# A graph transformer layer: when the edge histogram is built beside the keys and values, and when the last weight split and the attention row loads are issued

## The chip, the cores and the metric

The kernel runs on one core of a Trainium2 chip. The metric is the device time of the whole program in microseconds. The core has TensorE (PE, matrix products), VectorE (DVE), ScalarE (ACT), GpSimd (POOL) and the DMA queues, of which SyncE (SP) issues most. The engines run their own instruction lists in order and meet only at semaphores.

## The reference, cut to what matters

The layer takes 1250 nodes of 768 features and 41250 directed edges (self loops included). In outline:

```python
xn = layernorm(x)
# graph branch: two attention layers over the edges, src -> dst
h  = (layernorm(xn, g, b) @ W1).reshape(n, 4, 192)
e  = leaky_relu(s_src[src] + s_dst[dst], 0.2)
alpha = exp(e - segment_max(e)) / segment_sum(...)
out1 = segment_sum(alpha * h[src], dst) ; out2 = same with W2
gnn  = concat(x, out2) @ Wu + bu
# linear attention branch
q, k = elu(xn @ Wq + bq) + 1, elu(xn @ Wk + bk) + 1 ;  v = xn @ Wv + bv
kv = sum_n k v ; mix = (q kv / (q sum k)) @ Wo + bo
x = x + gnn + mix
x = x + mixture_of_experts(layernorm(x))      # top 2 of 8
```

## The kernel before, in words

All rows of x are cut into NT = 10 tiles of 128 rows, and features into KC = 6 blocks of 128. Large products are done in three half-precision passes: each operand is split into a high and a low part, so `product` (line 1931) issues 18 matmuls for one half of a tile. The high part of a weight is made by ScalarE (`high`, line 971), the low part by VectorE (`stage_low`, line 1330), each in CUTS = 3 pieces.

The edges are turned into a dense 1280x1280 table of counts, `CT`, by a histogram. The edges come in NU = 81 units of 512. For each unit VectorE writes four pairs of one-hot matrices (lines 1394 and 1395), TensorE multiplies them (four matmuls, line 2032) and VectorE adds the result of 240 columns to a window of `CT` (`edges_add`, line 1387). VectorE's order is fixed: after the one-hots of unit u it adds unit u-2, and it waits there for TensorE. The ring of one-hots has OB = 4 places. On TensorE unit u waits for the one-hots of u and for the add of u-2, since two PSUM banks (4 and 5) are used in turn.

The units are laid between the steps of two stages by `spread(step)`:

- **The key and value stage** has KV_STEPS = 36 steps. In round t (0 to 9) TensorE does two half products of values of tile t, two half products of keys of tile t+2, each followed by one step of units, and then 12 small matmuls that add k times v (line 2043). FIRST names the first step that takes units, KVU how many of the 81 are done in this stage. VectorE does in the same rounds the units, `key_biased` (line 1344, out of the banks of the keys), `key_features` (lines 1349, 1350), the low parts of expert weights (`conv_low`, line 1335) and from round 4 on a low part of the folded weight `MG` (line 1425). Tile 1 of the keys sits in banks 4 and 5 until `key_biased(1)` has read it.
- **The G stage** has 20 half products, each with one step of the units that are left.

Then come six products by Wo (line 2100), and the query stage: for each j of 6, TensorE does a half product of queries (18 matmuls, 512 columns), small denominator products of the block before (`den`, line 2113, which wait for `QT` of that block) and turns a piece of the edge mask (line 2159). ScalarE makes exp and relu of the queries and a high part of an expert weight, VectorE makes `QT` (line 1511), the low part of the expert weight (line 1335) and, in blocks 0, 1 and 2, one piece each of the low part of Wu (line 1330). From block 4 on VectorE also takes row maxima (`maxima1`, line 1492), and the first of them waits for four broadcast loads of the attention rows from `as_d` (line 716). SP issues those loads after it has served the expert pieces of block 2 and a store of the mask. After the last block TensorE does the graph half products, the first of which stands before `den(5)`.

The order of the work is written out by hand. No planner is in it.

Of the kernel before, what the change touches and what calls it, by code (L numbers as in the profile page):

```python
# [23 lines left out]
def gps_layer(nc, x, src, dst, norm_g, norm_b, W1, a_src1, a_dst1, b1, W2, a_src2, a_dst2, b2, Wu, bu,  # L24
# [27 lines left out]
    with ctx:  # L52
# [371 lines left out]
        s_k_biased = sem("k_biased")  # L424
# [86 lines left out]
        s_y_ready = sem("y_ready")  # L511

        KV_STEPS = 4 * NT - 4
        KVU = 54
        assert KVU <= NU
        xs_in = (s_x0_in, s_x1_in, s_x2_in, s_x3_in, s_x4_in, s_x5_in)
        convs_in = (s_ring0_in, s_ring1_in, s_ring2_in, s_ring3_in)
# [14 lines left out]
        CONST = 10  # L532
        CUTS = 3
        BLANK = 3600
        FIRST = 2
        AHEAD = 4
        FIRST_AT = {0: (4,), 1: (5, 6), 2: (7, 8), 3: (9, 10), 4: (11,)}
        KEY_AT = {4: (0, 0), 5: (0, 1), 6: (1, 0), 7: (1, 1)}
# [41 lines left out]
        def _(sp):  # L580
# [126 lines left out]
            for n, (c0, w) in enumerate(CH):  # L707
                for j in range(KC):
                    i = n * KC + j
                    convs(conv_of_j[i])  # L710
                    mask_stores(HALF_J.get(i, ()))
                    if i == CUTS - 1:
                        sp.wait_ge(s_cols_out, 16)
                        sp.wait_ge(s_stage_low, 4 * CUTS)
                        for h in range(H1):
                            sp.dma_start(arow1[h], as_d[h * NP:(h + 1) * NP].partition_broadcast(P)).then_inc(s_arow_in, 16)
                if n == len(CH) - 1:
                    sp.wait_ge(s_cols_ready, 2)
                    sp.dma_start(rr_d.rearrange("(r p) -> r p", p=P), rowst[0:2 * H1 * NT, :]).then_inc(s_cols_out, 16)
                    sp.wait_ge(s_max_done, H1 * NT)  # L720
                    sp.dma_start(WUB[0:KS], Wu[D:D + CW, :].rearrange("(k p) n -> p k n", p=KS)).then_inc(s_w2_in, 16)
                    sp.wait_ge(s_small_in, 96)
                    sp.dma_start(WUB[KS:KS + 1, 0, :], bias_d.rearrange("(a n) -> a n", a=1)).then_inc(s_w2_in, 16)
                    for b in (2, 3):
                        sp.wait_ge(convs_out[b], CONVS[b])
                    sp.dma_start(reg(O_G, 2 * GW), g_d[:, 0:2 * GW]).then_inc(s_gbuf0, 16)
                    sp.wait_ge(s_cols_out, 32)
                    rr_load(0)
                t0 = c0 // P
                for t in range(t0, (c0 + w) // P):  # L730
                    convs(conv_of_t[t])
                    if t == t0:
                        if t:
                            xa_load(t + 1)
                        continue
                    if t == t0 + 1:
                        xa_store(t0)
                    mask_stores(HALF_T.get(t, ()))
                    if t < NT - 1:
                        xa_load(t + 1)  # L740
                    else:
                        sp.wait_ge(s_zq_ready, NJ)
                        rr_load(1)
                        for b in range(2):
                            sp.wait_ge(masks_out[b], 16 * ((NT + 1 - b) // 2))
                        sp.wait_ge(xa_out[0], XAS)
                        sp.dma_start(reg(O_G + 2 * GW, 3 * GW), g_d[:, 2 * GW:5 * GW]).then_inc(s_gbuf1, 16)
                    xa_store(t)
# [476 lines left out]
        def _(dve):  # L1225
# [65 lines left out]
            with dve.If(some > 0):  # L1291

                with dve.Fori(0, NWIN) as w:
# [17 lines left out]
                    with dve.Fori(0, NU) as u:  # L1311
                        dve.wait_ge(s_left_step, w * LW + LW)
                        for j in range(EJ):
                            V.tensor_scalar(ohleft[:, j, :], iota[:, 0:P], kc[:, 1, j, bass.ds(u, 1)], None, ALU.is_equal)
                            i = V.tensor_scalar(ohk[:, 0, j, :], iota[:, 0:NT * W], kc[:, 0, j, bass.ds(u, 1)], None, ALU.is_equal)
# [189 lines left out]
            for n, (c0, w) in enumerate(CH):  # L1505
                for j in range(KC):
                    i = n * KC + j
                    dve.wait_ge(s_q_act, i + 1)
                    if c0:
                        dve.wait_ge(s_acc_psum, c0 // P)  # L1510
                    V.scalar_tensor_tensor(QT[:, j, 0:w], EQ[:, i % 3, 0:w], 1.0, RQ[:, i % 2, 0:w],
                                           ALU.min, ALU.add).then_inc(s_q_ready, 1)
                    for c in conv_of_j[i]:
                        conv_low(c)
                    if i < CUTS:
                        stage_low(3, i)
                    if i in IND_J:
                        edge_or_not(IND_J[i])
                    if j < KC - 1:
                        maxima1(MAX_J.get(i, ()))  # L1520
                    if i == NJ - KC + 1:
                        columns1()

                t0 = c0 // P
                dve.wait_ge(s_den_psum, 2 * n + 1)
                nt = w // P
                heads = recip[:, 0:nt, :]
                link(V.reciprocal(heads, ps[2][:, 0:nt * 2 * KC].rearrange("p (t h) -> p t h", t=nt)))
                for r in range(3):
                    part = rcols[:, 0:nt, 2 * KC * r:2 * KC * (r + 1)]  # L1530
                    k = V.tensor_copy(part, heads)
                    if r < 2:
                        link(k)
                        link(V.tensor_tensor(heads, heads, part, ALU.subtract))
                k.then_inc(s_den_ready, 1)
                for c in conv_of_t[t0]:
                    conv_low(c)
                late_maxima = MAX_J.get(n * KC + KC - 1, ())
                maxima1(late_maxima[0:1])
                dve.wait_ge(s_den_psum, 2 * n + 2)  # L1540
                V.tensor_copy(rparts[:, 0:w], ps[2].bitcast(BF16)[:, 2 * P:2 * P + w]).then_inc(s_den_ready, 1)
                maxima1(late_maxima[1:])

                def zq_low(i):
                    dve.wait_ge(s_zqh_ready, i + 1)
                    V.tensor_tensor(ZQ[:, i % KC, 1, 0:w], EQ[:, i % 3, 0:w], ZQ[:, i % KC, 0, 0:w], ALU.subtract).then_inc(s_zq_ready, 1)

                for j in range(KC):
                    i = n * KC + j
                    dve.wait_ge(s_bc_psum, i + 1)  # L1550
                    if j == 0:
                        dve.wait_ge(s_q_ready, (n + 1) * KC)
                    elif j >= 3:
                        dve.wait_ge(s_zq_ready, i - 2)
                    V.tensor_tensor(EQ[:, i % 3, 0:w], QT[:, j, 0:w], ps[i % 2][:, 0:w], ALU.mult).then_inc(s_z_ready, 1)
                    if j:
                        zq_low(i - 1)
                zq_low(n * KC + KC - 1)

                def acc_out(t):  # L1560
                    dve.wait_ge(s_acc_psum, t + 1)
                    dve.wait_ge(xa_in[t % 2], 16 * (t // 2 + 2))
                    for c in range(2):
                        h = slice(c * HALF, (c + 1) * HALF)
                        k = V.scalar_tensor_tensor(XA[t % 2][:, h], ps[4 + 2 * (t % 2) + c][:, 0:HALF], 1 / UP, XA[t % 2][:, h], ALU.mult, ALU.add)
                    k.then_inc(s_acc_ready, 1)

                for t in range(t0, (c0 + w) // P):
                    if t > t0:
                        for c in conv_of_t[t]:  # L1570
                            conv_low(c)
                    if t in IND_T:
                        edge_or_not(IND_T[t])
                    ns = list(MAX_T.get(t, ()))
                    if t == t0 + 1:
                        maxima1(ns[0:2])
                        acc_out(t0)
                        maxima1(ns[2:])
                    else:
                        maxima1(ns)  # L1580
                    if t == NT - 1:
                        dve.wait_ge(s_mask_psum, 2 * NT)
                        dve.wait_ge(s_rows_ready, 1)
                        V.memset(h2x[:, :, :, C2:C2 + 1], 1.0)
                        for u in range(NT):
                            i = V.tensor_copy(h2x[:, u, :, 0:C2], b1row.rearrange("p (h c) -> p h c", h=H2))
                        i.then_inc(s_col_ready, 1)
                    if t > t0:
                        acc_out(t)
# [334 lines left out]
        def _(pe):  # L1924
# [122 lines left out]
            for t in range(NT):  # L2047
                if t == 0:
                    pe.wait_ge(s_xnt_ready, NT)
                    pe.wait_ge(s_stage_low, 2 * CUTS)  # L2050
                elif t < NT - 1:
                    pe.wait_ge(s_v_ready, t)
                else:
                    pe.wait_ge(s_k_biased, NT)
                at_t = 4 * t if t < NT - 1 else 4 * t - 2
                for c in range(2):
                    i = product(ps[value_bank(t) + c][:, 0:HALF], xnt(t * P, (t + 1) * P), cols(WV, c * HALF, (c + 1) * HALF))
# [2 lines left out]
                    edges(at_t + c)  # L2060
                k = t + 2
                if k < NT:
                    pe.wait_ge(s_k_biased, k)
                    for c in range(2):
                        i = product(ps[key_bank(k) + c][:, 0:HALF], xnt(k * P, (k + 1) * P), cols(WK, c * HALF, (c + 1) * HALF))
                        if c:
# [400 lines left out]
```

## Time and profile before

| what | value |
|---|---|
| median of 3 runs | 996.6 us (994.78 to 998.07) |
| the profiled execution | 998.07 us |
| its span | 996.3 us |
| PE busy | 923.9 us (93%) |
| DVE busy | 754.2 us (76%) |
| ACT busy | 355.3 us (36%) |
| POOL busy | 127.4 us (13%) |
| mean granted clock of TensorE | 0.968 |

The profiled execution is the slowest of the three, 1.5 us over the median; 1.8 us of it lie outside the span. Busy time is what the hardware profiler recorded for each engine, and the share is of the span. A granted clock of 1.00 is 2.4 GHz, 0.50 is 1.2 GHz.

### The profile page before, as it was taken

What the parts mean: (1) busy time and instruction counts of PE and PEld (TensorE: products, weight loads), DVE (VectorE), ACT (ScalarE), POOL (GpSimd) and SP (SyncE); (2) the same over time, 40 slices, a digit from 0 to 9 for tenths busy, and PEclk for the clock granted to TensorE, in tenths of its full rate; (3) what the DMA queues carried; (4) which work ended last, traced back from release to release, by engine and by line L of the source; (5) the groups of instructions that cost most, each with busy time, mean ns of one, the idle gap of its engine ahead of it and who ended that gap; (6) DMA issues with size and microseconds to landing.
All of it is one profiled execution on the core that took longest, in us unless ns stands there. A gap on an engine that the chain in (4) does not pass through costs nothing.

```text
span 996.3 us, 17419 instructions
## 1 busy us (share of the span) xinstructions
PE 923.9 (93%) x6467; PEld 682.5 (69%) x6469; DVE 754.2 (76%) x1703; ACT 355.3 (36%) x474; POOL 127.4 (13%) x147
## 2 busy tenths in 40 slices
PE   6899999999999999999799999659998889999994
PEld 6667666666655555667599999558866656666662
DVE  7888999996966878794699998699989634444442
ACT  5751121313264225413245544135637222222230
POOL 3400000000010000000000000000010244554541
PEclk9999999999999999999899999979998799999998
DMA  9611121272468475486691100034085568778860
GB/s 328 195 35 51 62 81 49 80 270 114 160 207 275 140 245 163 134 293 199 230 422 71 53 1 1 0 125 209 3 316 204 208 193 203 182 182 202 192 163 4
DMA packets 61468, 155.45 MB, mean 156 GB/s; under 512 B 11956, under 2 KB 31286, under 8 KB 58442
## 3 DMA queue, kind: packets, MB, share of 16 engines
q1 hardware_dynamic: 47034, 112.32, 31.9%
q0 software_dynamic: 9936, 34.23, 13.8%
q10 hardware_dynamic: 4416, 7.78, 2.1%
q8 instruction: 54, 0.88, 0.4%
q14 instruction: 28, 0.23, 0.1%
HBM read 108.34 MB, written 48.94 MB: 158 GB/s over the span
## 4 chain that ended last, share of the span: by engine, by line
PE 73%; DVE 19%; issue 3%; DMA 2%; ACT 1%; DVEq 1%; SPq 0%; POOLq 0%; ACTq 0%
PE PS L1931 47%; PE PS L2220 14%; PE PS L2032 3%; DVE arena L1596 3%; DVE arena L1668 3%; DVE arena L1602 3%; PE PS L2392 2%; DVE arena L1330 1%; PE PS L2274 1%; PE PS L2043 1%; DMA arena<-as_d 1%; PE PS L2407 1%; DVE arena L1395 1%; PE PS L2113 1%; PE PS L2100 1%
## 5 line engine op out<-in xcount | busy, mean ns | idle before, releaser
L1931 PE MATMUL PS<-arena 128*128 128x384 f16 (+7 forms) x3396 | 562.0, 321 | 6.5 <-DVE arena L1921 3.0
L1931 PEld LDWEIGHTS PS<-arena 128*128 128x128 f16 (+2 forms) x3396 | 319.4, 98 | 210.5 <-issue 9.3
L2220 PE MATMUL PS<-arena 128*128 128x193 f32 (+1 forms) x1200 | 182.0, 313 | 9.8 <-DVE arena L1602 9.7
L2220 PEld LDWEIGHTS PS<-arena 128*128 128x128 f32 x1200 | 179.1, 192 | 12.8 <-DVE arena L1602 6.5
L1109 ACT ACTIVATE arena<-arena,AS 128x1250 f32<-128x1250 f32 x60 | 80.3, 1339 | 91.7 <-DVE arena L1596 91.4
L1602 DVE SCALAR_TENSOR_TENSOR arena<-arena 128x1250 f32<-128x1250 f32 x60 | 87.3, 1455 | 4.4 <-PE PS L2220 4.2
L1596 DVE SCALAR_TENSOR_TENSOR arena<-arena,AS 128x1250 f32<-128x1250 f32 x60 | 90.5, 1510 | 0.0
L1395 DVE TENSOR_SCALAR arena<-arena 128x240 f16<-128x240 f16 x324 | 88.9, 274 | 0.0
L1394 DVE TENSOR_SCALAR arena<-arena 128x128 f16<-128x128 f16 x324 | 79.9, 247 | 0.1
L1920 DVE SCALAR_TENSOR_TENSOR arena<-PS,arena 128x768 f32<-128x768 f32 x27 | 25.8, 957 | 61.2 <-PE PS L1931 61.2
L1219 ACT ACTIVATE arena<-PS 128x1536 f16<-128x1536 f16 x27 | 39.2, 1450 | 75.9 <-PE PS L2392 75.9
L1492 DVE CUSTOM_DVE_ANT_0 arena<-arena 128x1250 bf16<-128x1250 f32 x40 | 58.3, 1457 | 5.2 <-DMA arena<-as_d 4.4
L910 POOL DMA_INDIRECT out_dram<-arena x27 | 43.3, 1603 | 85.8 <-DVE arena L1921 66.1
L1335 DVE SCALAR_TENSOR_TENSOR arena<-arena 128x768 f16<-128x768 f32 x48 | 45.9, 967 | 6.2 <-ACT arena L976 5.9
L1387 DVE TENSOR_TENSOR arena<-arena,PS 128x240 f32 x81 | 32.3, 399 | 18.9 <-PE PS L2032 12.6
L1898 DVE SCALAR_TENSOR_TENSOR arena<-PS,arena 128x384 f32<-128x384 f32 x27 | 15.0, 557 | 40.5 <-PE PS L1931 35.2
L2032 PE MATMUL PS<-arena 128*128 128x240 f16 x324 | 42.6, 267 | 2.5 <-DVE arena L1387 2.5
L1005 ACT ACTIVATE arena<-arena 128x768 f32<-128x768 f32 x10 | 8.3, 843 | 100.1 <-DVE arena L1344 100.1
L976 ACT ACTIVATE arena<-arena 128x768 f16<-128x768 f32 x48 | 39.7, 838 | 7.8 <-DMA arena<-in_L_ffn_W_dram 7.8
L1213 ACT ACTIVATE arena<-arena 128x384 f32<-128x384 f32 x27 | 14.1, 522 | 72.1 <-DVE arena L1898 72.1
L2032 PEld LDWEIGHTS PS<-arena 128*128 128x128 f16 x324 | 31.5, 98 | 11.3 <-DVE arena L1395 3.1
L895 POOL DMA_INDIRECT arena<-xf_d,arena x27 | 26.7, 989 | 62.6 <-DVE arena L1873 54.6
(272 smaller groups left out, 931.3 us busy)
## 6 DMA issues: line engine op xcount, KB each, us to landing
arena<-in_L_ffn_W_dram SPq DMA_DIRECT2D x48, 384.0 KB, 3.8
fr_d<-arena SPq DMA_DIRECT2D x48, 384.0 KB, 3.0
arena<-fr_d SPq DMA_DIRECT2D x16, 1152.0 KB, 14.3
arena<-in_x_dram SPq DMA_DIRECT2D x18, 384.0 KB, 5.8
arena<-rr_d SPq DMA_DIRECT2D x4, 1280.0 KB, 8.8
g_d<-arena SPq DMA_DIRECT2D x10, 388.0 KB, 2.4
acc_d<-arena SPq DMA_DIRECT2D x10, 384.0 KB, 3.2
xf_d<-arena ACTq DMA_DIRECT2D x10, 384.0 KB, 3.4
```

The lines of the kernel that those rows point to most:

```text
L910: g.indirect_dma_start(out=out, out_offset=bass.IndirectOffsetOnAxis(ap=found[:, i:i + 1].bitcast(U32), axis=0), in_=Yb[:, i % 2, :], in_o ...
L976: a.activation(cbuf[b][:, PIECE:PIECE + PIECE // 2].bitcast(F16), cbuf[b][:, 0:PIECE], ACT.Copy, scale=UP).then_inc(s_conv_high, 1)
L1109: a.activation(BUF[:, unit % 3, 0:N], BUF[:, unit % 3, 0:N], ACT.Exp, bias=AS2[:, h, t:t + 1]).then_inc(s_e_ready, 1)
L1335: V.scalar_tensor_tensor(buf[:, 0:PIECE // 2].bitcast(F16), buf[:, 0:PIECE], UP, buf[:, PIECE:PIECE + PIECE // 2].bitcast(F16), ALU.mult, ...
L1394: V.tensor_scalar(ohlo[:, u % OB, j, :], iota[:, 0:P], kc[:, 1, j, u:u + 1], None, ALU.is_equal)
L1395: i = V.tensor_scalar(ohk[:, u % OB, j, :], iota[:, 0:NT * W], kc[:, 0, j, u:u + 1], None, ALU.is_equal)
L1492: V.tensor_tensor_reduce(out=junk1[:, 0:N], in0=arow1[h][:, 0:N], in1=mask1[d % 2].rearrange("p t d -> p (t d)")[:, 0:N], scale=1.0, scala ...
L1596: V.scalar_tensor_tensor(BUF[:, unit % 3, 0:N], RR[:, h % 2, 0, 0:N], AS8[:, h, t:t + 1], RR[:, h % 2, 1, 0:N], ALU.add, ALU.max).then_inc ...
L1602: V.scalar_tensor_tensor(PT[i % deep][:, 0:N], BUF[:, unit % 3, 0:N], 2.0, CT[:, t, 0:N], ALU.min, ALU.mult).then_inc(s_p_ready, 1)
L1931: m = T.matmul(out, left[i][x], right[i][y], start=first and i + r == 0, stop=last and 3 * i + r == n - 1)
L2032: i = T.matmul(ps[4 + u % 2][:, 0:NT * W], ohlo[:, u % OB, j, :], ohk[:, u % OB, j, :], start=j == 0, stop=j == EJ - 1)
L2220: m = T.matmul(ps[sum_bank(h, b)][:, r * (C + 1):(r + 1) * (C + 1)], PT[i % deep][:, d * P:(d + 1) * P], feats, start=t == 0 and r == 0, s ...
```

## The change

KVU goes from 54 to 58 and FIRST from 2 to 4, so that steps 4 to 35 take 58 units where steps 2 to 35 took 54, and the G stage takes 23 where it took 27. TensorE's wait for `key_biased(1)` moves from the keys of tile 2 (round 0) to the start of round 1, ahead of the first unit. In the query stage VectorE makes all three low pieces of Wu in block 0, ahead of that block's `conv_low`, and SP issues the four row loads after block 1 in place of block 2.

```diff
-        KVU = 54
+        KVU = 58
...
-        FIRST = 2
+        FIRST = 4
...
                     mask_stores(HALF_J.get(i, ()))
-                    if i == CUTS - 1:
+                    if i == 1:
                         sp.wait_ge(s_cols_out, 16)
                         sp.wait_ge(s_stage_low, 4 * CUTS)
                         for h in range(H1):
...
+                    if i == 0:
+                        for q in range(CUTS):
+                            stage_low(3, q)
                     for c in conv_of_j[i]:
                         conv_low(c)
-                    if i < CUTS:
-                        stage_low(3, i)
...
                 else:
                     pe.wait_ge(s_k_biased, NT)
+                if t == 1:
+                    pe.wait_ge(s_k_biased, 2)
...
                 k = t + 2
                 if k < NT:
-                    pe.wait_ge(s_k_biased, k)
+                    if k > 2:
+                        pe.wait_ge(s_k_biased, k)
```

## Rows read from the trace of the kernel before

**Rows 1.** The page: the chain that ended last, shares of the span by engine.

```profile
PE 73%; DVE 19%; issue 3%; DMA 2%; ACT 1%; DVEq 1%; SPq 0%; POOLq 0%; ACTq 0%
```

**Rows 2.** Busy time by stretch: length, busy PE, PEld, DVE, ACT, POOL, clock, DMA.

```profile
72.72:203.48 130.76, 128.18 (x882) 87.67 (x881) 123.08 (x511) 26.80 (x42) 0.00 (x0) 0.99 0.20 64
```

**Rows 3.** Timeline of PE, key and value stage: start, length, what, [idle before <- releaser].

```profile
62.18 8.94 PE L1931 MATMUL PS<-arena 128*128 128x384 f16 x54 [1.17 <-DVE arena L1330]
...
76.45 3.09 PE L1931 MATMUL PS<-arena 128*128 128x384 f16 x18
79.38 0.57 PE L2032 MATMUL PS<-arena 128*128 128x240 f16 x4
...
197.65 0.57 PE L2032 MATMUL PS<-arena 128*128 128x240 f16 x4 [1.33 <-DVE arena L1387]
199.38 0.88 PE L2032 MATMUL PS<-arena 128*128 128x240 f16 x4 [1.16 <-DVE arena L1387]
200.06 4.50 PE L1931 MATMUL PS<-arena 128*128 128x384 f16 x18
204.39 0.98 PE L2032 MATMUL PS<-arena 128*128 128x240 f16 x8
205.21 2.85 PE L2043 MATMUL PS<-arena 128*128 128x129 f32 x24
207.90 3.12 PE L1931 MATMUL PS<-arena 128*128 128x388 f16 x18
...
278.72 7.91 PE L2100 MATMUL PS<-arena 128*128 128x384 f32 x24
```

**Rows 4.** Timeline of DVE in the same stage.

```profile
72.72 0.41 DVE L1387 TENSOR_TENSOR arena<-arena,PS 128x240 f32 x1 [0.60 <-issue]
...
119.33 0.40 DVE L1387 TENSOR_TENSOR arena<-arena,PS 128x240 f32 x1
...
121.06 0.39 DVE L1387 TENSOR_TENSOR arena<-arena,PS 128x240 f32 x1
...
193.28 0.56 DVE L1349 TENSOR_SCALAR arena<-arena 128x768 f32<-128x768 f32 x1 [0.91 <-ACT arena L1005]
...
203.17 0.40 DVE L1387 TENSOR_TENSOR arena<-arena,PS 128x240 f32 x1
```

**Rows 5.** Busy time by stretch behind two waits of PE, columns as rows 2.

```profile
200.00:202.00 2.00, 2.00 (x9) 0.91 (x8) 2.00 (x12) 0.00 (x0) 0.00 (x0) 0.50 0.35 122
322.00:324.00 2.00, 2.00 (x10) 0.97 (x8) 1.83 (x7) 0.00 (x0) 0.00 (x0) 0.59 0.75 224
```

**Rows 6.** Timeline of DVE in the query stage.

```profile
293.73 0.96 DVE L1335 SCALAR_TENSOR_TENSOR arena<-arena 128x768 f16<-128x768 f32 x1
294.60 2.47 DVE L1330 SCALAR_TENSOR_TENSOR arena<-arena 128x1536 f16<-128x1536 f32 x1
...
299.88 1.75 DVE L1330 SCALAR_TENSOR_TENSOR arena<-arena 128x1536 f16<-128x1536 f32 x1
...
316.87 1.46 DVE L1492 CUSTOM_DVE_ANT_0 arena<-arena 128x1250 bf16<-128x1250 f32 x1 [4.41 <-DMA arena<-as_d]
...
319.76 0.69 DVE L1511 SCALAR_TENSOR_TENSOR arena<-arena 128x512 f32<-128x512 f32 x1
```

**Rows 7.** Timeline of PE in the query stage.

```profile
299.32 0.95 PE L2113 MATMUL PS<-arena 128*128 128x2 f32 x8
...
320.50 1.05 PE L2113 MATMUL PS<-arena 128*128 128x2 f32 x8 [2.37 <-DVE arena L1511]
321.41 4.76 PE L1931 MATMUL PS<-arena 128*128 128x384 f16 x18
```

**Rows 8.** Timeline of SP: the issue of the four row loads.

```profile
304.94 2.38 SPq L716 DMA_DIRECT2D arena<-as_d  x4
```

**Rows 9.** The tile of the row loads: their time to landing.

```profile
DMA to landing us min/median/max: 6.0/8.3/9.8
```

**Rows 10.** Timeline of POOL in the query stage.

```profile
294.37 4.78 POOL L846 TENSOR_SCALAR_AFFINE_SELECT arena<-arena 128x768 bf16<-128x768 bf16 x3
```

## The prediction, made before the changed kernel was built or run

> **What bounds the kernel now.** I read the chain first. It runs on TensorE for 73% of the span and on VectorE for 19% [rows 1], so the questions are where PE waits for DVE in the edited stages and what each wait costs. In the key and value stage the PE timeline shows one place near its end: waits of 1.33 and 1.16 us before units 50 and 51 (counting from 0), both for the add on L1387 [rows 3]. Behind them 18 matmuls of 384 columns take 4.50 us where such a group takes 3.09 [rows 3], and the granted clock there is 0.50, which is 1.2 GHz [rows 5]. So this place costs 2.5 + 1.4 = 3.9 us. The reader is to see next that DVE is nearly full there: from its first add (72.72) to the add that frees the last unit of the stage (203.17) lie 130.76 us with 123.08 busy [rows 2, 4]. Only 7.68 us are idle. In the query stage PE waits 2.37 us for `QT` (L1511) before `den(5)`, and DVE had itself waited 4.41 us for the row loads from as_d [rows 6, 7]. The group behind is again slow, 4.76 against 3.09 us, at a clock of 0.59 [rows 3, 5, 7]. This place costs 2.37 + 1.67 = 4.0 us. Elsewhere in the edited stages PE is without a gap of note.
>
> **The change, part 1: the units.** PE's own work is only moved. Eight matmuls of two units take 0.82 us (204.39 to 205.21), so one takes 0.41 [rows 3], and the four units moved out of the G stage take 1.64 us with them: the G stage, 70.82 us long (207.90 to 278.72, rows 3), becomes 69.2. What matters is DVE's side. A unit costs it 1.73 us (from the add at 119.33 to the one at 121.06, rows 4).
>
> DVE's list from the add of unit 0 to the add that frees the last unit (51 before, 55 now) is the same but for four more units: 123.08 + 4 x 1.73 = 130.0 us busy. It also starts later. Round 0 loses its three units, so round 1 begins on PE at 76.45 - 3 x 0.41 = 75.22. Unit 0 now follows the first half product of values: in before that unit group starts 2.93 us after 76.45 and lasts 0.57 [rows 3], so here it ends at 75.22 + 2.93 + 0.57 = 78.7. The add of unit 0 starts at about 78.8, where it started at 72.72 [rows 4]. DVE cannot run ahead meanwhile: it makes the one-hots of units 0 to 2 and then stands at that add with everything of its list behind it, keys' bias and features included. PE isn't held by that at first.
>
> The end of the list is 78.8 + 130.0 plus what DVE still idles. From below this is the 0.91 us it waits for ScalarE's exp in round 8 [rows 4], which stays: 209.7. From above it is all 7.68 us: 216.5. I take 1.4 us idle and 210.2, near the lower end, because an engine that is behind finds PE's results ready; the idle time of before lay where DVE was ahead. In before this point is 203.17 + 0.31 = 203.48. Behind it come now the last unit, 0.41, and two groups of k times v, 2.69 (205.21 to 207.90, rows 3), with 0.1 to pass the semaphore: 213.4. PE again waits in front of units 54 and 55 and drops to the half clock. Its last half product is then 1.4 us longer, but DVE still has two units and a `conv_low` (0.87) to do, 4.3 us, beside which 2.9 + 0.4 us of PE run; so some 0.5 of the 1.4 shows. The G stage starts at 213.9 against 207.90, and the products by Wo at 213.9 + 69.2 = 283.1 against 278.72. I take **+4.5 us**; the bounds are 209.7 without the clock (+3.4) and 216.5 (+10.2).
>
> Moving the wait for `key_biased(1)` costs nothing: that instruction is done before DVE's first add, long before PE begins round 1 at 75.2. In the G stage DVE has one unit less in every fifth step and more idle time than before, so nothing is late there. `MG`'s last low part follows the last add by 0.9 us, inside the 3.2 us that PE still has.
>
> **Part 2: the low part of Wu.** In block 0 DVE has made `QT(0)` by 293.73 and then does `conv_low`, one piece of Wu, `QT(1)`. Now three pieces stand ahead of both. A piece takes 1.75 us alone, but 2.47 at 294.60, beside POOL's three selects [rows 6, 10]. Operations overlap by some 0.08 (the `conv_low` of 0.96 at 293.73 has the next start after 0.87), so a piece counts 1.67, a `conv_low` 0.87 and a `QT` 0.6. Between 294.60 and 299.88 stand one of each, 3.1 us of work in 5.28: each lost 0.7. The selects hang on a transfer, not on DVE, and stay where they are. So `QT(1)` starts at 293.73 + 3 x 1.67 + 0.87 + (2 or 3) x 0.7 = 301.0 to 301.7 and ends 0.69 later [rows 6]. `den(1)` stood at 299.32 [rows 7] and waits for it: 2.4 to 3.1 us of new PE idle time. Without any loss to POOL it would be 1.0. The two known waits of 2.4 us and of 2.5 us in two parts were followed by the half clock [rows 3, 5, 7], a wait of 1.17 was not (54 matmuls in 8.94 us, rows 3). So I add 1.5 for the clock: **+4.2 us** (bounds 1.0 and 3.1 + 1.7 = 4.8). ScalarE passes, since its next expo needs `QT(1)` only with the queries of block 3. SP is held: it serves the first expert piece 5.6 us later; its next loads have blocks to spare.
>
> The Trainium skill (SBUF — State Buffer, "SBUF: two separate sides") says of the port pair that VectorE and GpSimd share that whichever of them starts first has it for the whole instruction and the other fully blocks. The trace shows less: DVE gets through three operations, losing 2.1 us in all, while the selects run for 4.78 us (294.37 to 299.15) [rows 6, 10]. By that rule the pieces after the first would wait until 299.15, and `QT(1)` would end at 299.15 + 2 x 1.67 + 0.87 + 0.69 = 304.1; the wait of PE would be 4.7 us instead of 2.4 to 3.1.
>
> **Part 3: the row loads.** SP now issues them behind the two transfers of the expert piece of block 1, whose low part is ready at 302.4 + 0.87 = 303.3. With 0.6 us for each of these issues (the four loads took 2.38) they go out from 304.5, against 304.94 [rows 8]: hardly earlier in absolute time. But PE and DVE come later by the new wait. DVE is ready for its first maximum at 316.87 - 4.41 = 312.46 before and at 315.2 or later now; the loads land within 9.8 us [rows 9] of an issue that ends at 306.9, at 316.7 in the worst case. Two maxima (2.9) and `QT(5)` (0.69) then end at 320.4. `den(5)` would have stood at 318.13 and now stands at 320.9 or later. The wait goes, and its clock loss with it: **-4.0 us**. The next on PE's path, the chain behind `den(5)`, has a half product of 3 us as cover.
>
> **Sum:** 4.5 + 4.2 - 4.0 = +4.7 us. The stages behind are bound as before and move as a whole. Against the profiled execution's 998.07 that is 1002.8; that execution is 1.5 us above the median of the runs, so I state 996.6 + 4.7 = **1001.3 us**. Its own range is +3.4 to +7 and -3.0 to +0.8 for the two stages, so 997.0 to 1004.4.
>
> **The rivals.**
>
> 1. The four units fit into DVE's idle time (7.68 against 6.9 us). Then the key and value stage is bound by PE throughout, its 3.9 us vanish, and with parts 2 and 3 near +0.2 the time is 992.9. It decides if DVE can run its one-hots ahead during round 0. For it: the ring has four places. Against: the order in which the add of u-2 stands behind the one-hots of u allows three units, and the idle time lay early, at just the units that are now gone. Chance 0.12.
> 2. The two parts cancel: part 2 costs its lower bound of 1.0 us, with no clock loss, since short waits don't bring it, and part 1 its lower 3.4 to 4: 3.7 + 1.0 - 4.0 = +0.7, 997.3. For it: one short wait passed without a drop. Against: the slowed rows beside POOL. Chance 0.17.
> 3. DVE's backlog costs PE more than the end: waits spread over rounds 4 to 8, each with `MG`, two expert pieces and seven units, hold `key_biased` up as well, and the clock falls several times. Part 1 goes toward its upper bound, say +8, and the time is 1004.8. It decides if the backlog reaches PE before round 7. For it: rounds 1 to 8 now hold about seven units each in place of six, 1.6 us more of DVE against 0.4 more of PE, where DVE was already busy for 94% of the time [rows 2]. Against: when DVE binds, slow matmuls hide behind it. Chance 0.07.
> 4. The selects block DVE as a whole: +1.7 us over the forecast or more, 1003.3. Chance 0.06. It is the page's rule above, as a mechanism here.
>
> My forecast has 0.58.
>
> **How the numbers follow.** A change under 0.3% (3 us) can't be told from none here: runs of before spread over 3.3 us. Of the forecast 0.03 falls inside that band; of rival 2 0.13 does, with 0.02 on each side; rivals 3 and 4 are slower, rival 1 is faster. Slower: 0.55 + 0.02 + 0.13 = 0.70. Same: 0.16. Faster: 0.12 + 0.02 = 0.14. The range goes from 997.3 (rival 2) less the spread of a median, 996.8, up to 1005.3, past rivals 3 and 4; it leaves out rival 1 and the far side of 3.
>
> **What would show it.** G's first product starts 5 to 7 us later than 207.90, and the products by Wo 4 to 5 us later than 278.72. DVE's busy share between its first add and the add of unit 55 is near 99%. The waits of PE for L1387 sum to more than the 2.5 us of before, the longest at units 54 and 55. `den(1)` waits 2.4 to 3.1 us for L1511 and a slow group of 512 columns follows; DVE's wait for as_d is gone and `den(5)` waits for nothing. I am wrong in part 1 if the products by Wo start by 281, in part 2 if PE has no wait over 1.5 us around 300, and in part 3 if a wait for as_d stays.

## The result

| | median of runs | profiled execution | span | granted clock |
|---|---|---|---|---|
| before | 995.69 us (994.35 to 998.07, 4 runs) | 998.07 us | 996.3 us | 0.968 |
| after | 1003.37 us (1002.69 to 1006.16, 4 runs) | 1002.98 us | 1001.2 us | 0.972 |

The change makes the kernel slower: ratio 1.008 with a 95% interval of 1.0051 to 1.0108. The forecast was 1001.3 us in a range of 996.8 to 1005.3. The profiled execution of the kernel before is the slowest of its four runs; that of the changed kernel is not among its four and lies 0.4 us under their median.

The timeline of PE of the changed kernel shows where. The columns are start, length, instruction, and idle time before it with what ended it. Lines moved: L1932 is the L1931 of before, L2033 the L2032, L2104 the L2100.

```profile
61.98 11.86 PE L1932 MATMUL PS<-arena 128*128 128x384 f16 x72 [1.17 <-DVE arena L1330]
...
77.94 0.57 PE L2033 MATMUL PS<-arena 128*128 128x240 f16 x4
...
140.16 0.57 PE L2033 MATMUL PS<-arena 128*128 128x240 f16 x4 [1.02 <-DVE arena L1387]
...
205.91 0.57 PE L2033 MATMUL PS<-arena 128*128 128x240 f16 x4 [2.12 <-DVE arena L1387]
207.65 0.96 PE L2033 MATMUL PS<-arena 128*128 128x240 f16 x4 [1.17 <-DVE arena L1387]
208.40 4.29 PE L1932 MATMUL PS<-arena 128*128 128x384 f16 x18
...
216.03 3.12 PE L1932 MATMUL PS<-arena 128*128 128x388 f16 x18
...
285.22 7.91 PE L2104 MATMUL PS<-arena 128*128 128x384 f32 x24
```

The granted clock fell behind the wait at 207.65 as it did in [rows 5] (columns as in [rows 2], the clock is the third number from the end):

```profile
208.00:210.00 2.00, 2.00 (x9) 1.03 (x7) 2.00 (x10) 0.00 (x0) 0.00 (x0) 0.50 0.21 77
```

The timeline is to be held against [rows 3]. G's first product starts at 216.03 where it started at 207.90, and the products by Wo at 285.22 where they started at 278.72. The stage itself began 0.2 us earlier in this execution (61.98 against 62.18), so the stage and G together cost 6.7 us more. The prediction's signs had 5 to 7 us for the first start and 4 to 5 for the second: they come 8.1 and 6.5 us later, so both are missed on the far side. The waits of PE for the add sum like this (first the changed kernel, then the kernel before, 60 to 350 us; columns: waiter, releaser, us in total, times, longest):

```profile
PE PS L2033 <- DVE arena L1387: 7.0, 8, 2.1
PE PS L2117 <- DVE arena L1511: 2.9, 1, 2.9
```

```profile
PE PS L2032 <- DVE arena L1387: 2.5, 2, 1.3
PE PS L2113 <- DVE arena L1511: 2.4, 1, 2.4
```

Once, at 200.69, PE also waits 0.3 us for `key_biased` (L1344).

The busy time by stretch shows DVE as the bound of the stage, from its first add to the one that frees the last unit, now 55 (columns as in [rows 2]):

```profile
79.70:211.73 132.03, 124.69 (x851) 83.42 (x850) 129.51 (x547) 26.68 (x42) 0.00 (x0) 0.99 0.19 64
```

It is busy for 98% of that stretch, where [rows 2] gave 94%. Its idle time fell from 7.7 to 2.5 us.

In the query stage the wait for the row loads is gone and another has come. First DVE, then PE of the changed kernel; they answer to [rows 6, 7]:

```profile
300.10 6.51 DVE L1330 SCALAR_TENSOR_TENSOR arena<-arena 128x1536 f16<-128x1536 f32 x3
306.53 1.65 DVE L1335 SCALAR_TENSOR_TENSOR arena<-arena 128x768 f16<-128x768 f32 x1
308.11 0.68 DVE L1511 SCALAR_TENSOR_TENSOR arena<-arena 128x512 f32<-128x512 f32 x1
...
323.67 1.46 DVE L1492 CUSTOM_DVE_ANT_0 arena<-arena 128x1250 bf16<-128x1250 f32 x1
```

```profile
308.84 1.05 PE L2117 MATMUL PS<-arena 128*128 128x2 f32 x8 [2.85 <-DVE arena L1511]
...
310.21 5.55 PE L1932 MATMUL PS<-arena 128*128 128x512 f16 x18
...
333.00 0.39 PE L2124 MATMUL PS<-identb,arena 128*128 128x128 bf16 x4
```

`den(1)` waits 2.85 us, and the group behind takes 5.55 us where the others of its kind take 4.05. The first maximum (L1492) waits for nothing. SP issued the row loads at 311.84, which is 26.6 us behind the start of Wo's products, against 26.2 before: they didn't go out earlier. DVE comes to the maximum later, 38.5 us behind that start where before it stood ready after 33.7. From Wo's products to the first `den_turned` it takes 47.8 us, 47.3 before: the query edits cancel in this pair to 0.5 us. At `den_turned` the changed kernel is 7.0 us late (333.00 against 326.01) and at the last product of the second attention layer 7.5 (726.72 against 719.25). Behind it this pair of executions differs the other way: at the first transposes in the experts (L2407 before, L2411 after) the changed kernel is only 4.8 us late (805.24 against 800.46), and the two spans differ by 4.9 us while the medians differ by 7.7. No edit lies in that phase, and what differs there stays open.

### The profile page after: what moved, and what is told of

Its sections match the earlier page's. It is cut to its first block, busy times and chain, and to the rows that moved or that the text cites. A ratio compares the mean times of both kernels' runs of the same rounds, so it can differ in the third digit from the quotient of the medians.

```text
span 1001.2 us, 17419 instructions
## 1 busy us (share of the span) xinstructions
PE 923.8 (92%) x6467; PEld 679.6 (68%) x6469; DVE 753.9 (75%) x1703; ACT 354.7 (35%) x474; POOL 130.8 (13%) x147
## 4 chain that ended last, share of the span: by engine, by line
PE 73%; DVE 20%; issue 2%; DMA 2%; ACT 1%; DVEq 1%; POOLq 0%; SPq 0%
PE PS L1932 47%; PE PS L2224 14%; PE PS L2033 3%; DVE arena L1597 3%; DVE arena L1669 3%; DVE arena L1603 2%; PE PS L2396 2%; DVE arena L1330 2%; PE PS L2044 1%; PE PS L2117 1%; DVE arena L1395 1%; PE PS L2411 1%; PE PS L2278 1%; DVE stats L1796 1%; DVE arena L1822 1%
## 5 line engine op out<-in xcount | busy, mean ns | idle before, releaser
L1932 PE MATMUL PS<-arena 128*128 128x384 f16 (+7 forms) x3396 | 562.0, 321 | 6.9 <-DVE arena L1922 3.0
L1932 PEld LDWEIGHTS PS<-arena 128*128 128x128 f16 (+2 forms) x3396 | 319.1, 98 | 212.0 <-issue 10.0
L1395 DVE TENSOR_SCALAR arena<-arena 128x240 f16<-128x240 f16 x324 | 91.1, 281 | 0.0
L1394 DVE TENSOR_SCALAR arena<-arena 128x128 f16<-128x128 f16 x324 | 82.1, 253 | 0.1
L1492 DVE CUSTOM_DVE_ANT_0 arena<-arena 128x1250 bf16<-128x1250 f32 x40 | 58.4, 1459 | 0.8
L2033 PE MATMUL PS<-arena 128*128 128x240 f16 x324 | 43.9, 267 | 7.0 <-DVE arena L1387 7.0
L2033 PEld LDWEIGHTS PS<-arena 128*128 128x128 f16 x324 | 30.8, 98 | 18.0 <-DVE arena L1395 9.0
```

Of the source, the lines that this page charges most:

```text
L1394: V.tensor_scalar(ohlo[:, u % OB, j, :], iota[:, 0:P], kc[:, 1, j, u:u + 1], None, ALU.is_equal)
L1395: i = V.tensor_scalar(ohk[:, u % OB, j, :], iota[:, 0:NT * W], kc[:, 0, j, u:u + 1], None, ALU.is_equal)
L1492: V.tensor_tensor_reduce(out=junk1[:, 0:N], in0=arow1[h][:, 0:N], in1=mask1[d % 2].rearrange("p t d -> p (t d)")[:, 0:N], scale=1.0, scala ...
L1932: m = T.matmul(out, left[i][x], right[i][y], start=first and i + r == 0, stop=last and 3 * i + r == n - 1)
L2033: i = T.matmul(ps[4 + u % 2][:, 0:NT * W], ohlo[:, u % OB, j, :], ohk[:, u % OB, j, :], start=j == 0, stop=j == EJ - 1)
```

## The experiments

Each kernel is the kernel before with the edit shown, unless said otherwise. Stages are compared by two lengths, which free them from where an execution starts: A, from the first value product of the key and value stage to Wo's products (216.54 us before, 223.24 after), and B, from there to the first `den_turned` (47.29 before, 47.78 after). Both are read from one profiled execution of each kernel. Four of the kernels (FIRST alone, KVU alone, only the low pieces, the selects held back) were run in that one execution only, so they have no ratio; their times were 998.49, 1001.75, 998.30 and 998.05 us.

**Only the units.**

```diff
-        KVU = 54
+        KVU = 58
...
-        FIRST = 2
+        FIRST = 4
...
+                if t == 1:
+                    pe.wait_ge(s_k_biased, 2)
...
-                    pe.wait_ge(s_k_biased, k)
+                    if k > 2:
+                        pe.wait_ge(s_k_biased, k)
```

> Only the units are moved (KVU 58, FIRST 4, the wait for key_biased(1) in round 1); the query stage is as before. Theory A (VectorE's list of the key and value stage starts 7 us later and is 6.9 us longer, so it ends the stage): the first G product starts 8 us later than before (near 216), the products by Wo 6.5 us later (near 285.2), and the whole is slower by 6 to 7 us (1002 to 1003, ratio 1.006 to 1.007), nearly all of what the full change costs. Rival B (the query edits carry the loss and the units are moved for nothing): Wo starts within 1 us of 278.7 and the time is that of before.

Ratio 1.0071 (1.0047 to 1.0094), median 1003.7 against 996.05 us; A is 223.12 us. The units carry the loss; rival B falls. B is 48.82 us, 1.5 more than before, though nothing is edited there: the wait before `den(5)` is the same (2.36 us), and the half clock behind it lasts longer, the group taking 5.50 us where it took 4.76 [rows 7].

**Only the query stage.**

```diff
+                    if i == 0:
+                        for q in range(CUTS):
+                            stage_low(3, q)
                     for c in conv_of_j[i]:
                         conv_low(c)
-                    if i < CUTS:
-                        stage_low(3, i)
...
-                    if i == CUTS - 1:
+                    if i == 1:
```

> Only the query stage is edited (three low pieces of Wu in block 0, row loads behind block 1); the units are as before. Theory A: den(1) waits 2.8 us and a slow group of 512 columns follows (5.5 us against 4.05), the wait for the row loads (4.4 us on VectorE, 2.4 on TensorE) is gone, and the two cancel: den_turned of the first chunk, at 326.0 before, moves by 0 to +1 us, the ratio is 0.999 to 1.002. Rival B: the ratio is 1.006 or more.

Ratio 1.0021 (1.0003 to 1.0038), median 999.6 against 996.05 us: slightly slower, just past the upper edge of what was expected, and under rival B's. A is that of before (216.54). `den(1)` waits and the clock is half for longer here than in the changed kernel:

```profile
302.35 1.86 PE L2114 MATMUL PS<-arena 128*128 128x2 f32 x8 [2.86 <-DVE arena L1511]
...
304.56 6.27 PE L1932 MATMUL PS<-arena 128*128 128x512 f16 x18
...
328.08 0.39 PE L2121 MATMUL PS<-identb,arena 128*128 128x128 bf16 x4
```

B is 49.35 us, 2.1 over before, not within 1 us. The wait is the same to 0.01 us; what differs is the time at half clock.

**FIRST alone, and KVU alone.** The first takes FIRST = 4 with its moved wait and leaves KVU at 54, the second KVU = 58 and leaves FIRST at 2.

> FIRST 4 with its moved wait, but KVU stays 54 (54 units in 32 steps), query stage as before. If late start and longer list add up on VectorE: its first add starts at 79.7 as in the full change, the products by Wo start 2 to 3.5 us later than 278.7. If the number of units alone decides, they start at 278.7. If the start alone decides, they start near 285.

> KVU 58 with FIRST 2 and the waits of before, query stage as before. Additive account: VectorE's first add stays at 72.7, its list is 6.9 us longer, of which the 7.7 us of idle time take a part: the first G product 4 to 5 us later than 207.9, the products by Wo 2.5 to 3.5 us later than 278.7. If start alone decides: no change.

With FIRST alone DVE's first add is at 79.71, and A is 217.75 us: 1.2 longer, less than expected. With KVU alone the first add stays (72.63) and A is 221.83: 5.3 longer, more than expected. Most of both misses is the clock. The place behind the last two units, first with FIRST alone, then with KVU alone:

```profile
199.76 0.57 PE L2032 MATMUL PS<-arena 128*128 128x240 f16 x4 [2.00 <-DVE arena L1387]
201.49 0.57 PE L2032 MATMUL PS<-arena 128*128 128x240 f16 x4 [1.16 <-DVE arena L1387]
201.90 3.09 PE L1931 MATMUL PS<-arena 128*128 128x384 f16 x18
```

```profile
203.27 0.57 PE L2032 MATMUL PS<-arena 128*128 128x240 f16 x4 [2.12 <-DVE arena L1387]
205.00 0.96 PE L2032 MATMUL PS<-arena 128*128 128x240 f16 x4 [1.16 <-DVE arena L1387]
205.76 5.64 PE L1931 MATMUL PS<-arena 128*128 128x384 f16 x18
```

After nearly the same waits the group runs at full speed in one and takes 5.64 us in the other; in the kernel before it took 4.50 [rows 3]. The granted clock says the same, first with FIRST alone, then with KVU alone:

```profile
203.00:205.00 2.00, 2.00 (x15) 1.25 (x13) 2.00 (x12) 0.00 (x0) 0.00 (x0) 1.00 0.56 196
```

```profile
207.00:209.00 2.00, 2.00 (x8) 0.95 (x7) 2.00 (x11) 0.00 (x0) 0.00 (x0) 0.50 0.51 186
```

Taking the clock out shows the two parts. From the start of the second of these units to G's first product pass 7.42 us in all three executions without a drop there (FIRST alone, only the low pieces, the selects held back); with KVU alone it is 9.74, so the drop cost 2.3 us, and in the kernel before 8.52, so 1.1. The run with only the low pieces (next) has the units of before and no drop: its A is 215.47. Against that, FIRST alone costs 217.75 - 215.47 = 2.3 us, and KVU alone 221.83 - 2.32 - 215.47 = 4.0 us. Their sum is 6.3; both together cost 222.23 - 215.47 = 6.8 us without a drop (the run with the selects held back). So late start and longer list add up to within 0.5 us. The 4.0 us of KVU alone are still above the 2.5 to 3.5 expected, and not by the clock.

**Only the low pieces of Wu; the row loads stay behind block 2.**

> Only the three low pieces of Wu go into block 0; the row loads stay behind block 2. Theory: den(1) waits 2.8 us with the half clock behind it, and the VectorE wait for the row loads goes or shrinks all the same, because TensorE and VectorE arrive 4.4 us later while the loads, held only by block 2's expert piece, are issued about when they were (305 to 306): the move of the loads is worth under 1 us of TensorE. Rival: the earlier issue is what removes the wait, so that here PE again waits over 2 us before den(5).

The expectation failed in its second half, and the rival is nearly met (1.87 us where it had over 2). DVE waits for the loads as before and PE waits 1.87 us at `den(5)` on top of 2.85 at `den(1)` (first DVE and SP, then PE):

```profile
320.02 1.46 DVE L1492 CUSTOM_DVE_ANT_0 arena<-arena 128x1250 bf16<-128x1250 f32 x1 [3.92 <-DMA arena<-as_d]
```

```profile
307.21 2.55 SPq L716 DMA_DIRECT2D arena<-as_d  x4
```

```profile
301.19 1.05 PE L2114 MATMUL PS<-arena 128*128 128x2 f32 x8 [2.85 <-DVE arena L1511]
...
323.65 1.05 PE L2114 MATMUL PS<-arena 128*128 128x2 f32 x8 [1.87 <-DVE arena L1511]
```

The loads went out at 307.21, not at 305 to 306, and 3.4 us later than in before, counted from Wo's products: the expert pieces SP must serve first are late too. So with the pieces in block 0 it takes the edit of SP's order to avoid the second wait. B is 49.92 us, 2.1 more than in the changed kernel, and 1.87 of that is this wait.

**The full change, with GpSimd's selects held back** until `QT` of block 2:

```diff
             pool.wait_ge(s_small_in, 96)
+            pool.wait_ge(s_q_ready, 3)
             select(g.memset(spread_heads, 0.0))
```

> The full change, but GpSimd's selects wait until QT of block 2 is made (s_q_ready 3), so they run beside no low piece of Wu. If the selects cause the part of the new wait that is over 1 us: the three low pieces take 1.75 us each (5.1 us in a row against 6.5), den(1) waits 0.5 to 1.3 us instead of 2.85, and the granted clock behind it stays at 1.00. If they don't: three pieces still take 6.5 us, den(1) waits 2.8.

`den(1)` waits 0.73 us and nothing is slow behind it:

```profile
305.86 1.05 PE L2118 MATMUL PS<-arena 128*128 128x2 f32 x8 [0.73 <-DVE arena L1512]
307.05 4.05 PE L1933 MATMUL PS<-arena 128*128 128x512 f16 x18
```

B falls to 43.97 us, 3.8 less than in the changed kernel. The selects suffer from the collision as well. First POOL in the changed kernel, then here:

```profile
300.87 6.51 POOL L846 TENSOR_SCALAR_AFFINE_SELECT arena<-arena 128x768 bf16<-128x768 bf16 x3
```

```profile
308.31 3.03 POOL L847 TENSOR_SCALAR_AFFINE_SELECT arena<-arena 128x768 bf16<-128x768 bf16 x3 [0.15 <-POOL arena L844]
```

And DVE here, the three pieces and the `conv_low` behind them:

```profile
299.25 5.09 DVE L1331 SCALAR_TENSOR_TENSOR arena<-arena 128x1536 f16<-128x1536 f32 x3
304.25 0.95 DVE L1336 SCALAR_TENSOR_TENSOR arena<-arena 128x768 f16<-128x768 f32 x1
...
320.53 1.46 DVE L1493 CUSTOM_DVE_ANT_0 arena<-arena 128x1250 bf16<-128x1250 f32 x1 [1.44 <-DMA arena<-as_d]
```

Apart from each other the pieces and the `conv_low` take 5.95 us (299.25 to 305.20) and the selects 3.03, 8.98 in all. In the changed kernel the same seven operations lie between 300.10 and 308.18, in 8.08 us. So beside each other the two engines saved only 0.9 us against strict turns. A is 222.23 without a drop of the clock. The last row shows that the row loads come late for DVE again once the wait at `den(1)` is short; PE isn't held by it here.

**The low pieces put where DVE was idle:** two ahead of block 0, one in block 1, and the loads behind block 1.

```diff
+            for q in range(2):
+                stage_low(3, q)
             for n, (c0, w) in enumerate(CH):
...
                     for c in conv_of_j[i]:
                         conv_low(c)
-                    if i < CUTS:
-                        stage_low(3, i)
+                    if i == 1:
+                        stage_low(3, 2)
...
-                    if i == CUTS - 1:
+                    if i == 1:
```

> Units as before; two low pieces of Wu are made ahead of block 0's QT, where VectorE sat idle for 2.6 us, the third in block 1, and the row loads go out behind block 1. Theory: neither den(1) nor den(5) waits over 0.5 us; VectorE comes to its first maximum with the loads landed or within 1 us; den_turned of the first chunk starts 3.5 to 4 us earlier than 326.0, ratio 0.996. Rival (the loads can't land earlier, because the queue ahead of them is what holds them): den(5) still waits 2 us, ratio 0.999 to 1.0.

Ratio 0.9952 (0.9935 to 0.9969), median 992.21 against 996.38 us. B is 43.12 us, 4.2 less than before; neither `den(1)` nor `den(5)` waits.

```profile
290.15 3.42 DVE L1330 SCALAR_TENSOR_TENSOR arena<-arena 128x1536 f16<-128x1536 f32 x2
...
297.89 2.45 DVE L1330 SCALAR_TENSOR_TENSOR arena<-arena 128x1536 f16<-128x1536 f32 x1
...
312.35 1.45 DVE L1492 CUSTOM_DVE_ANT_0 arena<-arena 128x1250 bf16<-128x1250 f32 x1
```

The pieces at 290.15 fill the time in which DVE stood before `QT(0)`, and the loads (issued at 300.42) have landed when the maxima want them. They go out right behind the third piece (297.89 + 2.45 = 300.34). By its code SP holds these loads not only for its own earlier work but also for the last low piece of Wu (`sp.wait_ge(s_stage_low, 4 * CUTS)` in the block shown in the change). In the kernel before that piece is this one:

```profile
303.01 1.74 DVE L1330 SCALAR_TENSOR_TENSOR arena<-arena 128x1536 f16<-128x1536 f32 x1
```

It ended at 304.75 and the loads went out at 304.94 [rows 8], so a new order of SP alone could hardly have brought them forward; pieces and loads had to move together. No run parts the two.

**Fewer units at the end of the stage.**

```diff
-        KVU = 54
+        KVU = 51
+        EARLY, EARLY_END = 49, 32
...
+            if step < EARLY_END:
+                step, n = step - FIRST, EARLY_END - FIRST
+                return range(step * EARLY // n, (step + 1) * EARLY // n)
+            if step < KV_STEPS:
+                step, n, late = step - EARLY_END, KV_STEPS - EARLY_END, KVU - EARLY
+                return range(EARLY + step * late // n, EARLY + (step + 1) * late // n)
```

> Query stage as before; 49 units in steps 2 to 31, 2 in steps 32 to 35 and 30 in the G stage (KVU 51, FIRST 2). Theory (VectorE's backlog in the last two rounds is what TensorE waits for): no wait of TensorE for L1387 over 0.5 us, no half clock near 200, the products by Wo 3.5 to 4.2 us earlier than 278.7, ratio 0.996. Rival (VectorE is full over the whole stage, so thinning its end only moves the wait into G): VectorE is late in the G stage and Wo's products start no earlier than 278.

Ratio 0.9966 (0.9944 to 0.9989). No wait for the add is left near 200 and no half clock, and A is 213.73 us, 2.8 less than before: under the 3.5 to 4.2 expected. The rest is in G, where PE now waits 0.54 and 0.42 us for the add, so the rival holds for a part. The median is 993.49 against 996.38 us.

**Both together, and with one unit less in G** (KVU = 52, EARLY = 50).

> The edits of the two runs before together: low pieces of Wu ahead and row loads behind block 1, with 49 units in steps 2 to 31, 2 in steps 32 to 35, 30 in the G stage. Counted from the first value product, the products by Wo start 2.8 us earlier than in before and the first den_turned another 4.2 us: 7 us in all, ratio 0.993 (0.991 to 0.996). If the two gains share a cause, it is about 0.996.

> As the run beside it, but 50 units in steps 2 to 31 and 29 in the G stage (KVU 52). If VectorE's lateness in the G stage (two waits of TensorE, 0.96 us in all, with 30 units there) is what the thinned tail gave back, one unit fewer takes at least half of it away and Wo's products start 0.4 to 1 us earlier than there; if the key and value stage is at its limit again, a wait for L1387 near 200 comes back and they start later.

The first gives a ratio of 0.9954 (0.9938 to 0.9971) with A 213.77 and B 43.12 us: the stages gain the 7 us expected (2.8 + 4.2), so the two gains add up there. The ratio is inside the range expected, but its interval doesn't reach 0.993; by the medians the gain is 5.3 us. The second gives 0.9937 (0.9920 to 0.9954), median 989.28 against 996.57 us, the fastest kernel of this study. It beats the kernel before and the changed one. Its A is 213.93, so the stages did not get shorter by the unit, against the 0.4 to 1 us expected; of the two waits in G that of 0.55 us is gone and that of 0.42 stays, and one of 0.34 us near 91 is new. That the second is better than the first isn't shown.

## Why the prediction was right, and where it was short

The direction, the range and the mechanism held; the size was 4.7 us against 7.7 between the medians. The stated time was nearer (1001.3 against 1003.37) because the median of before came out 0.9 us lower than the one that the forecast was added to.

- **Part 1, the units (+4.5 us forecast, +6.7 measured).** This is the term that was mis-sized. The G stage of 69.2 us came out as 69.19. DVE's list was forecast at 130.0 us busy and measured 129.51. Its first add was forecast for 78.8 and came at 79.70, though the unit's matmuls ended at 78.51: the step that said "at about 78.8" left out 1.2 us that pass between them when DVE stands at the add. The trace of before had the same gap: unit 0's matmuls end at 70.95 + 0.57 = 71.52 and the add starts at 72.72 [rows 4], though DVE's own work ended at 72.11. The rows are, first of before and then of the changed kernel:

```profile
70.95 0.57 PE L2032 MATMUL PS<-arena 128*128 128x240 f16 x4
```

```profile
79.70 0.40 DVE L1387 TENSOR_TENSOR arena<-arena,PS 128x240 f32 x1 [7.79 <-issue]
```

  The list idled 2.5 us, not 1.4. Behind it came 4.3 us, not 3.7, with the clock. Together 0.9 - 0.5 + 1.1 + 0.6 = 2.1 us. FIRST alone and KVU alone (2.3 and 4.0 us without the clock) confirm that both edits count, as the sum had it. The 3.9 us that the prediction put on the old place near 200 were 2.5 of waits and 1.1 of clock on the path, not 1.4.
- **The moved wait costs nothing:** right. PE runs 72 matmuls from 61.98 without a gap.
- **Part 2, the low pieces (+4.2, 4.35 measured: 2.85 of wait and 1.5 of clock).** Right, and with its cause: with the selects held back the wait is 0.73 us, where the forecast put 1.0. The clock's share is not fixed: behind the same wait it was 2.2 us on the group alone in the run with the query edits only (6.27 against 4.05), and 1.7 with the low pieces only (5.74).
- **Part 3, the row loads (-4.0):** right in the full change, for the reason given: DVE comes later, the loads don't come earlier (the forecast had them 0.4 us earlier, counted from Wo's products they went out 0.4 us later). So the gain is in part the wait of part 2 in another place. The run with the low pieces alone corrects my later belief that the earlier issue did little: it is needed, since what SP serves before the loads is late as well.
- **Rival 1** (the units fit into idle time) fell with the run of the units alone. **Rival 2** (part 1 at its lower end, part 2 at 1.0 us) fell with both stages: 6.7 and 4.35 us. **Rival 3** was half right: PE waits eight times, from 90 us on, but the clock dropped only at the end. **Rival 4**, DVE wholly blocked by the selects, fell: 2.85 us of wait, not 4.7. Its working let the three selects block DVE as one. The Trainium skill (SBUF — State Buffer, "SBUF: two separate sides") has the later of the two wait for the whole instruction of the other, which, read for single instructions, leaves DVE a turn between two selects. An estimate for turns, from the rows of the run with the selects held back, is 0.73 + 3.03 = 3.8 us of wait. The trace comes near to turns but under them: 2.85 us, and 8.08 us for what needs 8.98 one after another. The measurement decides.

The first bullet's size in plain terms: 6.7 - 4.5 = 2.2 us of the 3.0 us by which the medians lie over the forecast. Of the other 0.8, the query stage has 0.3 (+0.5 us against +0.2); the rest is inside the spread of the runs.

## What to carry to other kernels

Before moving work between two stages, compare how full the *second* engine is in each: TensorE's work was only moved here, but VectorE was 94% busy in the stage that got more. The list started 7.2 us later (counted from the stage's start) and grew by 6.4 us, and VectorE's 7.7 idle microseconds took up only 5.2 of these 13.6. When a wait is blamed on a transfer, look for idle time of the engine whose work gates the transfer's issue; two pieces of work put into such a gap, the third in block 1 and the loads behind it gave 4.2 us, where all three pieces in block 0 only traded one wait for another. Measure stage lengths in the trace, not only the whole: two edits that cancel look like no edit.

## What the runs showed of the hardware that was not expected

The clock's answer to a short wait is not fixed. PE waited 1.3 and 1.16 us before the same two units in four executions with the units of before, and the group behind took 4.50, 4.77 and 4.33 us in three of them (the kernel before, the query edits alone, the low pieces ahead) and 3.09 in the fourth (the low pieces alone). With 2.12 and 1.16 us (1.17 in the first) it took 4.29, 4.23, 5.64 and 3.09 (the changed kernel, the units alone, KVU alone, the selects held back). The granted clock behind the waits was 0.50 wherever the group was slow and 1.00 where it took 3.09. Measured up to G's first product, a pair of waits of this kind cost between 0 and 2.3 us more than itself, and a difference of 2 us in one pair of profiles can be that alone. What decides between the two outcomes no run here shows.

A DVE operation of 1.75 us beside GpSimd's selects took 2.2 us on the mean of three, and the selects went from 1.0 to 2.2 us each. Both engines lose.
